# A decoder kernel on one core: an earlier load of k and q, and a chunk of attention scores split around two transposes

## The chip, the cores and the metric

One core of a Trainium2 chip runs the whole kernel. The metric is the device time of one execution in microseconds (us). A profiled execution adds a trace with the start and length of the instructions of each engine: TensorE (PE; its weight loads are PEld), VectorE (DVE), ScalarE (ACT), GpSimd (POOL) and the DMA queues of SyncE (SP, in rows SPq) and of ScalarE (ACTq). Times in rows count from the first instruction.

## What is computed

One decoder layer on x of 16 sequences x 256 tokens x 512, in float32. The first third is differential attention over the heads of one token (32 half-heads by 32, not over the sequence):

```
q = split(x @ Wq.T) * SCALE ; k = split(x @ Wk.T) ; v = heads(x @ Wv.T)
att = softmax(einsum('bnqd,bnkd->bnqk', q, k))
diff = att[:, :, :H, :H] - lam * att[:, :, H:, H:]
out = rms(einsum('bnah,bhnd->bnad', diff, v)) * (1 - LAM_INIT)
x = layernorm(x + out @ Wo.T + bo)
x = layernorm(x + x * scan(decay, ctx * ctx))
h = relu(x @ ternary(W_fc).T)**2 ; x = layernorm(x + rms_norm(h) @ ternary(W_proj).T)
```

The ternary weights (sign times a scale per group of 64) are also made in the kernel.

## The kernel before

The 4096 tokens are worked in 8 blocks of 512. The kernel has two phases; the change lies in the first, which takes the first 520 us or so. The second (output projection, scan, feed-forward) runs from then on.

**The first phase** is a software pipeline written out by hand, one list of steps for each engine, in `body(i, do_2, do_1)`: body 0 and 1 are written out, bodies 2 to 7 run as a loop (on SyncE the last one is written out too). In body i TensorE projects block i into q, k and v, computes the scores of block i-1, and mixes the values of block i-2. Beside these it transposes the ternary weights: part 0 (W_fc) of body i behind projections 8 and 9, part 1 (W_proj) at the start of body i+1. Engines wait on semaphores only.

TensorE's body, by the lines: `x_transpose(i, t)` (L531) transposes token tile t of x, for t of 0 to 3, into a bank of PSUM. There are two banks, used in turn, so tiles 2 and 3 wait until tiles 0 and 1 have been taken out: by ScalarE (`x_upper`, L837, the high part `xth`) and by VectorE (`x_lower`, L1040, the low part `xtl`). In L541 and L542 transpose t waits for the high and low parts of tile t-2. `scores(i, c, first, end)` (L565) does chunk c of four: for each of 32 groups a small matmul of k with a block-diagonal q (`qbd`). Chunks 0 and 1 need the first half of q, 2 and 3 the second; chunk 0 also needs k. A chunk fills two banks, and `s_ps` (L582) tells of it per column strip, at the chunk's last eighth group (gq == 7). `w_transpose(i-1, 1, 0)` (L604) waits for the low part of x tile 2. `project(i, n)` (L547) for n of 0 to 11 is 12 matmuls each; projection 0 waits for all four low parts.

The order in TensorE's body (L622) is transposes 0 and 1, score chunk 0, transposes 2 and 3, weight transpose, projection 0 with chunk 1 inside it, and so on; chunks 2 and 3 stand behind projections 5 and 7.

**The way of q and k.** ScalarE copies each projection out of PSUM (`f_copy`, L844) and writes it to DRAM from its own queue: q chunks are n of 0 to 3, k chunks 4 to 7, v chunks 8 to 11. The copy of chunk n waits for the write of chunk n-3. SyncE loads them back in another layout: `first_half_load(i)` (L397) holds until the scores of block i-1 are done (`s_ps`) and chunks 0, 1, 5, 6 and 7 are written, then issues one load of k (L387, 1 MB) and eight of q (L382, 64 KB each). `second_half_load` (L403) brings the rest of q.

**The way of the weights.** `w_in` is one buffer, filled twice in a body: with W_fc (L428, L436) and with W_proj (L441). The second fill has to wait until the weight transposes behind projections 8 and 9 have read the first. ScalarE's `w_round(i, 1)` (L874) reads it at the end of the body, behind the copy of chunk 11: absolute values to `w_b` (L880), then signs. VectorE's `w_signs(i, 1)` (L1128; L1142 to L1151) is the last step of its body (L1185), behind the softmax of chunk 3 and the turn of the difference. The next in its queue is `x_lower(i+1, 0)`. GpSimd multiplies (L1439).

**SyncE's body** (L424): the loads of the difference for block i-2, of the next x, of the second half of q, of W_fc, the writes of W_proj's transposes, the load of v; then, in L440 to L442, the hold for the weight transposes, the load of W_proj into `w_in` and `first_half_load(i)`; then the writes of W_fc's transposes (L445) and of o. A hold stops SyncE, and all that is behind it waits. Each issue takes its own time on SyncE.

Of the kernel before, what the change touches and what calls it, by code (L numbers as in the profile page):

```python
# [58 lines left out]
def at(i, per, k):  # L59

    return i * per + k
# [7 lines left out]
def later(i):  # L69

    return not (isinstance(i, int) and i == 0)
# [15 lines left out]
def program(nc, x_in, ctx_in, wq, wk, wv, wo, bo, lq1, lq2, lk1, lk2, decay, w_fc, w_proj, out):  # L87
# [15 lines left out]
    with ExitStack() as stack:  # L103
# [189 lines left out]
        FULL = G // 2  # L293
# [12 lines left out]
        def x_bank(t):  # L306

            return ps_t[:] if t % 2 == 0 else ps_f[:, 0, :]
# [41 lines left out]
        def _(sp):  # L350
# [15 lines left out]
            def hold(*waits):  # L366


                for n, (signal, value) in enumerate(waits):
                    if n and not isinstance(value, int):  # L370
                        sp.sem_inc(passed, 1)
                    sp.wait_ge(signal, value)
                if not isinstance(waits[-1][1], int):
                    sp.sem_inc(passed, 1)

            def f_written(i, chunks):

                return [(f_wr[n % 3], at(i, 64, 16 * (n // 3 + 1))) for n in chunks]

            def q_load(i, s):  # L380
                for t in range(LANES):
                    sp.dma_start(qbd[H * t:H * (t + 1), lane_slot(t), :, :],  # L382
                                 q_scr[i, s * 256:(s + 1) * 256, t * G:(t + 1) * G]
                                 .rearrange("(d a) g -> d a g", a=H)).then_inc(qbd_ld, 16)

            def k2_load(i):
                sp.dma_start(k2[:], k_scr[i].rearrange("t (d h) g -> (t d) h g", h=2 * H)).then_inc(k2_ld, 16)  # L387

            def v2_load(i):
                hold(*([(av_ps, at(i, 16, 0))] if later(i) else []),  # L390
                     *f_written(i, (9, 10, 11)))
                for t in range(LANES):
                    at_t = H * (2 * (t % 4) + t // 4)
                    sp.dma_start(v2[at_t:at_t + H, :, :],
                                 v_scr[i, t].rearrange("(h e) g -> h e g", e=HD)).then_inc(v2_ld, 16)

            def first_half_load(i):  # L397

                hold((s_ps, at(i, 16, 0)) if later(i) else (zeroed, 2), *f_written(i, (0, 1, 5, 6, 7)))
                k2_load(i)  # L400
                q_load(i, 0)

            def second_half_load(i):  # L403
                hold((s_ps, at(i, 16, 8)), *f_written(i, (2, 3)))
                q_load(i, 1)

            def dbd_load(i):

                hold((d_tr, i + 1))
                for t in range(LANES):  # L410
                    sp.dma_start(dbd[H * t:H * (t + 1), t, :, :],
                                 dt[H * t:H * (t + 1), :, :]).then_inc(dbd_ld, 16)

            def o_write(i):
                hold((o_done, at(i, 4, 4)))
                sp.dma_start(o_scr[i].rearrange("t (a e) g -> (t a) e g", e=HD), o_sb[:]).then_inc(o_wr, 16)

            def w2_write(i):
                for r in range(2):
                    hold((wt_ev, at(i, 4, r + 3)))  # L420
                    sp.dma_start(w2_scr[:, bass.ds(i * 2 + r, 1), :],
                                 w_st[:, r:r + 1, :]).then_inc(wt_wr[r], 16)

            def body(i, do_2, do_1, last=False):  # L424
                if do_2:
                    dbd_load(i - 2)
                if not later(i):
                    sp.dma_start(w_in[:].rearrange("p (r d) -> p r d", d=D), fc_t[i]).then_inc(wt_ld, 16)  # L428
                if not last:
                    hold((xt_ps, at(i, 4, 4)))  # L430
                    sp.dma_start(xa[:], x_t[i + 1]).then_inc(xa_ld, 16)
                if do_1:
                    second_half_load(i - 1)
                if later(i):
                    hold((wt_ps, at(i, 4, 0)))
                    sp.dma_start(w_in[:].rearrange("p (r d) -> p r d", d=D), fc_t[i]).then_inc(wt_ld, 16)  # L436
                    w2_write(i - 1)
                if do_1:
                    v2_load(i - 1)
                hold((wt_ps, at(i, 4, 2)))  # L440
                sp.dma_start(w_in[:].rearrange("p (b n) -> p b n", b=4), proj_t[i]).then_inc(wt_ld, 16)  # L441
                first_half_load(i)  # L442
                for r in range(2):
                    hold((wt_ev, at(i, 4, r + 1)))
                    sp.dma_start(w1_scr[:, :, bass.ds(i * 256 + r * P, P)],  # L445
                                 w_st[:, r, :].rearrange("p (k h) -> p k h", k=KC)).then_inc(wt_wr[r], 16)
                if do_2:
                    o_write(i - 2)

            body(0, False, False)  # L450
            body(1, False, True)
            with sp.Fori(2, NSB - 1) as i:
                body(i, True, True)
# [62 lines left out]
        def _(pe):  # L516
# [14 lines left out]
            def x_transpose(i, t):  # L531

                if t == 0:
                    pe.wait_ge(xa_ld, at(i, 16, 16))
                    if later(i):
                        pe.wait_ge(wt_ev, at(i - 1, 4, 2))
                elif t == 1:
                    if later(i):
                        pe.wait_ge(f_ev, at(i - 1, 12, 11))
                else:  # L540
                    pe.wait_ge(xt_hi, at(i, TT, t - 1))  # L541
                    pe.wait_ge(xt_lo, at(i, TT, t - 1))  # L542
                for k in range(KC):
                    last = nc.tensor.transpose(x_bank(t)[:, k * P:(k + 1) * P], xa[:, t, k * P:(k + 1) * P], ident[:])
                last.then_inc(xt_ps, 1)
# [19 lines left out]
            def scores(i, c, first, end):  # L565

                if first == 0:
                    if c % 2 == 0:
                        pe.wait_ge(qbd_ld, at(i, 256, 128 * (c // 2 + 1)))
                    if c == 0:  # L570
                        pe.wait_ge(k2_ld, at(i, 16, 16))
                    if c >= 2 or later(i):
                        pe.wait_ge(s_y, at(i, 4, c - 1))
                for n in range(first, end):
                    gq, j = n // 4, n % 4
                    g = j * 16 + (c % 2) * 8 + gq
                    last = nc.tensor.matmul(ps_s[32 * j:32 * (j + 1), 2 * (c % 2) + gq // 4,  # L577
                                                 (gq % 4) * P:(gq % 4 + 1) * P],
                                            k2[:, :, g], qbd[:, :, :, g].rearrange("p a b -> p (a b)"),
                                            start=True, stop=True)  # L580
                    if gq == 7:
                        last.then_inc(s_ps, 1)  # L582
# [39 lines left out]
            def body(i, do_2, do_1):  # L622
                x_transpose(i, 0)
                x_transpose(i, 1)
                if do_1:
                    scores(i - 1, 0, 0, FULL)
                x_transpose(i, 2)
                x_transpose(i, 3)
                if later(i):
                    w_transpose(i - 1, 1, 0)  # L630
                for n in range(12):
                    def beside(k):
                        if do_1 and n == 0 and k == 1:
                            scores(i - 1, 1, 0, FULL)

                    project(i, n, beside)
                    if do_2 and 1 <= n <= 4:
                        mix(i - 2, n - 1, 0, G // 4)
                    if do_1 and n in (5, 7):
                        scores(i - 1, n // 2, 0, FULL)  # L640
                    if n in W_FIRST:
                        w_transpose(i, 0, W_FIRST.index(n))
                    if n == W_SECOND and later(i):
                        w_transpose(i - 1, 1, 1)

            phase_a(pe, body)


# [838 lines left out]
```

## Time and profile before

| | us |
|---|---|
| median of 3 runs | 1276.65 |
| lowest, highest | 1274.16, 1279.75 |
| the profiled execution | 1274.55 |
| its span, first to last instruction | 1272.7 |
| TensorE matmuls busy | 1100.6 (86%) |
| VectorE busy | 939.4 (74%) |
| ScalarE busy | 587.1 (46%) |
| mean granted TensorE clock | 0.94 of full |

The time outside of the span is 1.85 us. Busy times are sums over the span, and say nothing on which wait ends last; for that one goes to the waits and the timelines of one body. A wait is put down to the releaser that came last. The granted clock of TensorE has two levels, 1.2 GHz (0.5) and 2.4 GHz (1.0); the mean of a stretch tells how much of it was at which.

### The profile page before, as it was taken

How to read it: one execution, taken by the hardware profiler on the slowest of the kernel's cores; microseconds unless marked ns; L12 is line 12 of the kernel's file. 1: busy time of each engine (PE TensorE's matmuls, PEld its weight loads, DVE VectorE, ACT ScalarE, POOL GpSimd, SP SyncE). 2: the span in 40 equal slices, each digit the busy share in tenths (PEclk: the TensorE clock that was granted, in tenths of full speed). 3: DMA queues.
4: the chain of work that ended last, by engine and by line, in shares of the span. 5: the costliest groups of instructions: out<-in, count | busy, mean ns of one | idle time of the engine just before them, and what ended most of it. 6: DMA issues, size and time to landing. Idle time of an engine off the chain costs nothing.

```text
span 1272.7 us, 22077 instructions
## 1 busy us (share of the span) xinstructions
PE 1100.6 (86%) x7424; PEld 873.7 (69%) x7424; DVE 939.4 (74%) x1932; ACT 587.1 (46%) x906; POOL 205.9 (16%) x202
## 2 busy tenths in 40 slices
PE   5988989889797979635599998998989989899995
PEld 4766767667575757424378787787877878778784
DVE  4287878787878888786858677696785867958746
ACT  4333333333243333310346555566555655655683
POOL 3100030303131312132140103003030030210000
PEclk9999999999898989767599999999999999999998
DMA  7566475766657565983530021201211012100001
GB/s 278 158 175 160 140 163 174 157 186 137 200 120 221 100 183 117 290 215 113 193 100 34 1 67 67 66 10 56 66 66 53 13 66 66 66 1 2 34 1 66
DMA packets 184334, 139.32 MB, mean 109 GB/s; under 512 B 140128, under 2 KB 152416, under 8 KB 180192
## 3 DMA queue, kind: packets, MB, share of 16 engines
q1 hardware_dynamic: 113120, 113.57, 31.8%
q10 hardware_dynamic: 71168, 25.17, 8.2%
q8 instruction: 25, 0.41, 0.1%
q14 instruction: 21, 0.17, 0.0%
HBM read 82.09 MB, written 52.43 MB: 106 GB/s over the span
## 4 chain that ended last, share of the span: by engine, by line
PE 66%; DVE 9%; ACT 7%; issue 7%; SPq 5%; DMA 4%; POOL 1%; ACTq 0%; DVEq 0%; POOLq 0%
PE ps_f L558 18%; PE ps_s L744 14%; PE ps_f L728 12%; PE ps_s L577 9%; PE ps_o L679 6%; DMA qbd<-q_scr 3%; SPq L382 3%; PE ps_o L597 2%; ACT h_sb L947 2%; DVE h_acc L1279 1%; ACT r_sb L941 1%; PE ps_t L619 1%; PE ps_f L679 1%; DMA w_raw<-in_L_attn_Wv 1%; ACT oth L919 1%
## 5 line engine op out<-in xcount | busy, mean ns | idle before, releaser
L728 PE MATMUL ps_f<-x2h,w 128*128 128x512 f32 x512 | 204.7, 400 | 1.6 <-DVE x2l L1260 1.6
L744 PE MATMUL ps_s<-w,hh 128*128 128x512 f32 x500 | 201.5, 403 | 0.0
L728 PE MATMUL ps_f<-x2l,w 128*128 128x512 f32 x512 | 200.7, 392 | 0.0
L744 PE MATMUL ps_s<-w,hl 128*128 128x512 f32 x500 | 199.3, 399 | 0.0
L1268 DVE TENSOR_TENSOR hl<-h_sb,hh 128x512 fp32r<-128x512 f32 x128 | 91.1, 712 | 112.2 <-ACT hh L951 110.5
L577 PE MATMUL ps_s<-qbd,k 128*32 128x128 f32 x2048 | 125.4, 412 | 55.0 <-DMA qbd<-q_scr 55.0
L558 PE MATMUL ps_f<-xth,wh 128*128 128x512 f32 x384 | 157.0, 409 | 1.6 <-DVE xtl L1044 1.6
L558 PE MATMUL ps_f<-xth,wl 128*128 128x512 f32 x384 | 150.3, 391 | 0.0
L558 PE MATMUL ps_f<-xtl,wh 128*128 128x512 f32 x384 | 149.8, 390 | 0.0
L577 PEld LDWEIGHTS ps_s<-qbd,k 128*32 128x32 f32 x2048 | 83.4, 149 | 91.9 <-issue 48.7
L1453 POOL TENSOR_TENSOR xb<-xb,bob 128x512 f32<-128x512 f32 x32 | 71.8, 2274 | 434.9 <-DMA xb<-in_x 434.9
L941 ACT ACTIVATE r_sb<-ps_f 128x512 f32<-128x512 f32 x128 | 76.2, 595 | 136.7 <-PE ps_f L728 136.5
L728 PEld LDWEIGHTS ps_f<-x2h,w 128*128 128x128 f32 x512 | 96.9, 189 | 21.1 <-issue 1.9
L744 PEld LDWEIGHTS ps_s<-w,hh 128*128 128x128 f32 x500 | 96.8, 194 | 19.9
L744 PEld LDWEIGHTS ps_s<-w,hl 128*128 128x128 f32 x500 | 96.7, 193 | 19.8
L728 PEld LDWEIGHTS ps_f<-x2l,w 128*128 128x128 f32 x512 | 96.8, 189 | 19.1
L959 ACT ACTIVATE h_sq<-h_sb 128x512 f32<-128x512 f32 x128 | 79.3, 620 | 55.3 <-DVE h_acc L1279 55.3
L851 ACT ACTIVATE f_sb<-ps_f 128x512 f32<-128x512 f32 x64 | 38.8, 606 | 135.9 <-PE ps_f L558 135.9
L558 PEld LDWEIGHTS ps_f<-xth,wh 128*128 128x128 f32 x384 | 72.1, 188 | 26.7 <-issue 11.9
L1439 POOL TENSOR_TENSOR w_in<-w_in,w_pos 128x512 f32<-128x512 f32 x32 | 37.6, 1196 | 291.3 <-DVE w_pos L1149 291.3
L947 ACT ACTIVATE h_sb<-r_sb 128x512 f32<-128x512 f32 x128 | 80.9, 632 | 6.4 <-ACT r_sb L941 2.8
L558 PEld LDWEIGHTS ps_f<-xth,wl 128*128 128x128 f32 x384 | 72.1, 188 | 16.1
(142 smaller groups left out, 1918.8 us busy)
## 6 DMA issues: line engine op xcount, KB each, us to landing
xa<-in_x SPq DMA_DIRECT2D x8, 1024.0 KB, 5.4
q_scr<-f_sb ACTq DMA_DIRECT2D x32, 256.0 KB, 2.6
k_scr<-f_sb ACTq DMA_DIRECT2D x32, 256.0 KB, 2.8
v_scr<-f_sb ACTq DMA_DIRECT2D x32, 256.0 KB, 5.7
k<-k_scr SPq DMA_DIRECT2D x8, 1024.0 KB, 7.5
qbd<-q_scr SPq DMA_DIRECT2D x128, 64.0 KB, 4.8
w_scr<-w_st SPq DMA_DIRECT2D x32, 256.0 KB, 4.9
v<-v_scr SPq DMA_DIRECT2D x64, 128.0 KB, 6.0
```

Source lines behind the costliest of these rows:

```text
L382: sp.dma_start(qbd[H * t:H * (t + 1), lane_slot(t), :, :], q_scr[i, s * 256:(s + 1) * 256, t * G:(t + 1) * G] .rearrange("(d a) g -> d a g ...
L558: last = nc.tensor.matmul(ps_f[:, n % 2, :], w[:, n // 4, k, cols], xx[:, k, :], start=(k == 0 and xx is xth and w is wh), stop=(k == KC - ...
L577: last = nc.tensor.matmul(ps_s[32 * j:32 * (j + 1), 2 * (c % 2) + gq // 4, (gq % 4) * P:(gq % 4 + 1) * P], k2[:, :, g], qbd[:, :, :, g].re ...
L679: last = nc.tensor.matmul(proj_bank(i, t), a[:, k, rows], w[:, k, :], start=(k == 0 and w is woh and a is oth), stop=(k == KC - 1 and a is ...
L728: last = nc.tensor.matmul(ps_f[:, j % 2, :], w1[:, k, j * P:(j + 1) * P], xx[:, k, :], start=(k == 0 and xx is x2h), stop=(k == KC - 1 and ...
L744: last = nc.tensor.matmul(ps_s[:, t, :], a[:, j % 4, t * P:(t + 1) * P], w2[:, j, :], start=(j == 0 and a is hh), stop=(j == HC - 1 and a ...
L851: nc.scalar.activation(f_sb[:, n % 3, :], ps_f[:, n % 2, :], ACT.Copy).then_inc(f_ev, 1)
L941: nc.scalar.activation(r_sb[:], ps_f[:, j % 2, :], ACT.Relu).then_inc(r_done, 1)
L947: nc.scalar.activation(h_sb[:, j % 4, :], r_sb[:], ACT.Square).then_inc(h_done, 1)
L959: nc.scalar.activation(h_sq[:, j % 2, :], h_sb[:, j % 4, :], ACT.Square).then_inc(hq_done, 1)
L1268: nc.vector.tensor_tensor(hl[:, j % 4, :], h_sb[:, j % 4, :], hh[:, j % 4, :].bitcast(F32), ALU.subtract).then_inc(hl_done, 1)
L1453: nc.gpsimd.tensor_tensor(xb[:, t, :], xb[:, t, :], bob[:], ALU.add).then_inc(xb_bias, 1)
```

## The change

SyncE issues the load of k and q (its hold included) ahead of the hold for the weight transposes and of the second load of `w_in`. TensorE does score chunk 0 in two halves of 16 groups: one ahead of x transposes 2 and 3, the other behind them. No instruction is added or removed.

```diff
@@ -437,9 +437,9 @@
                     w2_write(i - 1)
                 if do_1:
                     v2_load(i - 1)
+                first_half_load(i)
                 hold((wt_ps, at(i, 4, 2)))
                 sp.dma_start(w_in[:].rearrange("p (b n) -> p b n", b=4), proj_t[i]).then_inc(wt_ld, 16)
-                first_half_load(i)
                 for r in range(2):
                     hold((wt_ev, at(i, 4, r + 1)))
                     sp.dma_start(w1_scr[:, :, bass.ds(i * 256 + r * P, P)],
@@ -623,9 +623,11 @@
                 x_transpose(i, 0)
                 x_transpose(i, 1)
                 if do_1:
-                    scores(i - 1, 0, 0, FULL)
+                    scores(i - 1, 0, 0, FULL // 2)
                 x_transpose(i, 2)
                 x_transpose(i, 3)
+                if do_1:
+                    scores(i - 1, 0, FULL // 2, FULL)
                 if later(i):
                     w_transpose(i - 1, 1, 0)
                 for n in range(12):
```

## Rows read from the trace of the kernel before

**Rows 1.** Waits, bodies 2 to 7 (118 to 470 us): total, times, longest.
```profile
PE ps_s L577 <- DMA qbd<-q_scr: 39.6, 6, 7.5
...
PE ps_t L619 <- DVE xtl L1044: 7.1, 6, 1.3
```

**Rows 2.** TensorE, body 5: start us, us, what, idle before and its releaser.
```profile
299.18 3.92 PE L577 MATMUL ps_s<-qbd,k 128*32 128x128 f32 x64
...
315.02 0.60 PE L544 MATMUL ps_t<-ident,xa 128*128 128x128 f32 x4
315.46 0.60 PE L544 MATMUL ps_f<-ident,xa 128*128 128x128 f32 x4
323.61 3.92 PE L577 MATMUL ps_s<-qbd,k 128*32 128x128 f32 x64 [7.55 <-DMA qbd<-q_scr]
327.46 0.94 PE L544 MATMUL ps_t<-ident,xa 128*128 128x128 f32 x4
...
330.06 0.65 PE L619 MATMUL ps_t<-ident,w_in 128*128 128x128 f32 x4 [1.23 <-DVE xtl L1044]
```

**Rows 3.** Timeline of VectorE, body 5, same columns.
```profile
319.13 1.18 DVE L1142 TENSOR_REDUCE gsum<-w_b 128x16 f32<-128x1024 bf16 x1
...
324.28 0.69 DVE L1044 TENSOR_TENSOR xtl<-ps_t,xth 128x512 fp32r<-128x512 f32 x1
...
329.13 0.69 DVE L1044 TENSOR_TENSOR xtl<-ps_t,xth 128x512 fp32r<-128x512 f32 x1 [3.57 <-ACT xth L841]
```

**Rows 4.** Timeline of ScalarE, SP and ACT queues, end of body 4.
```profile
300.09 0.38 ACTq L860 DMA_DIRECT2D k_scr<-f_sb  x1
...
309.94 0.40 SPq L441 DMA_DIRECT2D w_in<-in_L_ffn_W_proj  x1
...
311.24 0.35 SPq L387 DMA_DIRECT2D k<-k_scr  x1
...
311.68 7.30 SPq L382 DMA_DIRECT2D qbd<-q_scr  x8
...
316.40 1.06 ACT L880 ACTIVATE w_b<-w_in 128x1024 bf16<-128x1024 f32 x1 [0.58 <-ACT f_sb L853]
```

**Rows 5.** DMA issues of 240 to 370 us: KB each, median us to landing.
```profile
k<-k_scr SPq DMA_DIRECT2D x2, 1024.0 KB, 8.1
...
k_scr<-f_sb ACTq DMA_DIRECT2D x8, 256.0 KB, 2.8
...
w_in<-in_L_ffn_W_fc SPq DMA_DIRECT2D x2, 512.0 KB, 5.0
```

**Rows 6.** Timeline, end of body 0 and start of body 1.
```profile
48.88 0.38 ACTq L860 DMA_DIRECT2D k_scr<-f_sb  x1
...
55.61 6.24 SPq L382 DMA_DIRECT2D qbd<-q_scr  x8
...
62.32 1.22 DVE L1142 TENSOR_REDUCE gsum<-w_b 128x16 f32<-128x1024 bf16 x1 [17.57 <-ACT w_b L880]
...
69.87 0.66 PE L544 MATMUL ps_t<-ident,xa 128*128 128x128 f32 x4
```

**Rows 7.** Timeline of TensorE, body 7, transposes 2 and 3.
```profile
459.49 1.11 PE L544 MATMUL ps_t<-ident,xa 128*128 128x128 f32 x4
460.40 0.99 PE L544 MATMUL ps_f<-ident,xa 128*128 128x128 f32 x4
```

**Rows 8.** Three stretches: us, engines busy, PEclk (granted clock), DMA share, GB/s.
```profile
300.00:310.00 10.00, 10.00 (x90) 7.71 (x83) 8.62 (x13) 2.91 (x4) 5.78 (x13) 1.00 0.23 52
321.00:328.00 7.00, 4.39 (x67) 3.23 (x68) 4.56 (x18) 0.00 (x0) 2.36 (x2) 0.52 0.98 299
328.00:331.00 3.00, 1.77 (x13) 1.44 (x12) 1.87 (x3) 1.26 (x3) 0.00 (x0) 0.99 0.43 75
```

**Rows 9.** Timeline of TensorE behind the loop.
```profile
526.35 1.09 PE L619 MATMUL ps_t<-ident,w_in 128*128 128x128 f32 x4 [1.68 <-POOL w_in L1439]
```

**Rows 10.** Chain that ended last, behind the loop: start us, us, what.
```profile
526.95 3.82 SPq L459
```

## The prediction, made before the changed kernel was run

> **What bounds the kernel now.** I read first who waits for whom in the six full bodies (2 to 7) [rows 1]: TensorE stands 39.6 us for q, six times, and 7.1 us for the low part of x before the weight transpose. Those 46.7 us, 7.8 us a body, are all that the change aims at.
>
> TensorE's timeline of body 5 shows where they lie [rows 2]. The second x transpose ends at 316.06 (315.46 + 0.60), the first score chunk starts at 323.61 after 7.55 us of idling for q, transposes 2 and 3 follow from 327.46 on, then 1.23 us idle, then the weight transpose at 330.06, with projection 0 behind it. From there TensorE has no gap until the next body's transposes. So what the change can move is what lies between the end of transpose 1 and the weight transpose: 14.0 us here.
>
> VectorE's timeline of the same stretch decides the case [rows 3]. It is not idle while TensorE is: from 319.13 on it makes the weights' signs; only then, at 324.28, does it make the low part of x tile 0, and right behind it that of tile 1. Transpose 2 waits for the first of these and transpose 3 for the second. Before the change the score chunk stood between, and neither wait showed.
>
> **Part 1, the load of k and q ahead.** Its hold (for the load at the end of body 4) needs the write of k chunk 7, issued at 300.09 [rows 4]; writes of k land in a median of 2.8 us [rows 5], so at 302.9. It also needs the last score chunk, which TensorE runs right behind projection 7, so at about the same time. Between the issue for w_in and that for k SP took 0.90 us for the holds (309.94 + 0.40 to 311.24), so with some 0.2 us for these scores k goes out at about 304.0 instead of 311.24: 7.2 us earlier. The eight q issues take 7.30 us in this body, to 311.7. The old chain from k's issue to the chunk's start was 12.4 us (311.24 to 323.61), so q is there at 316.4, when TensorE ends transpose 1 (316.06). The wait for q is gone, or 0.3 us of it is left.
>
> What is moved past: w_in's second load was issued at 309.94 and now stands behind nine issues, at about 311.8, with 1.5 MB in front of it. The nearest row is the first w_in load, issued right behind eight q loads: 5.0 us to landing [rows 5], so 316.8. ScalarE began to read w_in at 316.40 [rows 4] and its result (1.06 us) was ready at 317.46, but VectorE took it up only at 319.13 [rows 3]. There is 1.67 us of slack, and 0.4 is used: I cost this at nothing in bodies 2 to 7. The bounds are nothing (it can't gain, being issued later) and 1.8 us a body if w_in takes the 8.1 us that k takes [rows 5]. The weight writes and the write of o behind it on SP were held by q's issues before and are released as early or earlier. In the ACT queue, the write of v chunk 8 now runs beside k's load; the copy of chunk 11 waits for it, within the same slack.
>
> In body 1 the slack isn't there [rows 6]: VectorE stood idle for 17.57 us until ScalarE had read w_in, so it started the signs at 62.32. SP can start k at 51.7 there (48.88 + 2.8), the q issues take 6.24 us, w_in goes out at 58.3 and lands at 63.3; read in 1.1 us, it lets the signs start at 64.4, 2.1 us later. x tile 0's low part ends 5.84 us behind their start in body 5 (319.13 to 324.97), so at 70.3. Transpose 2 moves from 69.87 to about 70.5, and what stands between it and the weight transpose grows from 2.6 us (body 5: 327.46 to 330.06 [rows 2]) to 3.86 (1.9 us for the transposes at the low clock, told below, and 1.96 for the half chunk): 0.6 + 1.3 = **+1.9 us**. If w_in lands in the 2.8 us of a k write, it is about 0.
>
> **Part 2, the halves.** A chunk is 3.92 us [rows 2], so a half is 1.96. New body 5: first half 316.1 to 318.0; then TensorE waits for the low part of tile 0, done at 324.97 (324.28 + 0.69), plus 0.24 us, which is what passed between such an end (329.82) and the weight transpose (330.06). Idle: 325.2 - 318.0 = 7.2 us. VectorE's chain hangs on TensorE's projection 10 by way of ScalarE, so I take it as the same in all six bodies. The second half now covers the low parts of tiles 2 and 3, and the 1.23 us wait goes. At an equal clock: 6 x 7.2 = 43.2 us of idling against 46.7, less 0.1 us a body for transpose 3, which waits for tile 1: **-2.9 us**. The wait for q is thus not removed; VectorE takes it over almost whole.
>
> The clock then takes that back. The windows show it near half (0.52, the 1.2 GHz level) from 321 to 328 us and full (2.4 GHz) behind [rows 8]: it was low after TensorE had idled some 5 us, and back 4.5 us after it resumed. Before, the work done at the low clock was mostly scores, and a chunk of those takes 3.92 us at either level (at 323.61, and at 299.18 [rows 2] with the clock full [rows 8]). Now the idling lies directly ahead of transposes 2 and 3. Body 7 shows their price at the low clock: 459.49, 460.40, end 461.39, so 1.9 us for the pair [rows 7]; 1.04 us for transposes 0 and 1 at the full one (315.02 to 316.06 [rows 2]). That is +0.8; the weight transpose (0.65 us; 1.09 at the low clock [rows 9]) and the first matmuls of projection 0 come 3.8 us after resumption, when the clock may or may not be back: +0.35, some half of the full price. Six bodies: 6.9, less 1.2 that is paid already (body 7's pair 0.86, body 5's transpose 2 with 0.94 instead of 0.60, 0.34): **+5.7 us**.
>
> The Trainium skill has a rule that speaks against this placing (TensorE: Matmul & The Clock Gate, section "HAM oscillation"): a short burst of matmuls in front of a long wait doesn't keep the clock up, and the work behind the wait starts cold every time. By it the sum is as told; without it 5.7 us less. The trace agrees in body 5, with its 0.52.
>
> **Behind the loop.** The last score chunk 0 also stops waiting for q, but what follows it waits for GpSimd's weights (1.68 us, until 526.35 [rows 9]) and then for SP's long row of issues [rows 10]. These begin with the write of o, released by GpSimd, and no part of it is moved. The nearest stall that may ease, since k and q have landed earlier, is the 3.82 us issue at 526.95: bounds 0 and -1.9 (half of it). I take **-0.7 us**. The second phase runs the same instructions.
>
> **Sum:** 1.9 - 2.9 + 5.7 - 0.7 = +4.0 us. The profiled execution took 1274.55 us (span 1272.7), so 1278.6 by its own time; it lies 2.1 us under the median of 1276.65, and on the median the forecast is **1280.6 us**, 0.3% slower. Effects under 0.5% (6.4 us) are about what a measurement of this kernel can't tell from no change.
>
> **The rivals.**
> *The clock costs nothing* (the half chunk shortens the cold stretch, or it ends before the transposes). For it: it was back in body 5 by the time of the second of these transposes. Then body 1 costs 1.1, and the sum is -2.9 + 1.1 - 0.7 = -2.5: 1274. With body 1 at no cost and the whole of the bound behind the loop, -4.8: 1272.
> *w_in becomes the wait* (the other side, slower). Place: SP's second w_in load, read by ScalarE, on which VectorE's signs hang, and on those transposes 2 and 3. It decides from the point where w_in lands later than 318.1 in body 5 (316.40 + 1.67). At k's 8.1 us it lands at 319.9: 1.8 us late, six times 10.8 us, and in body 1 3.1 more: 1276.65 + 4.0 + 10.8 + 3.1 = 1295; half of that lateness gives 1288. Against it: w_in has half of k's bytes.
> [...]
> *VectorE is not in the way* (the waits for x's low parts come earlier than I read, so that the stalls really go). Then only the 2.4 us from a transpose to the end of its low part (327.46 to 329.82) would stay in each body, and 46.7 - 14.4 = 32 us would go: 1244. Against it stands the order of VectorE's queue; what is open is a partial form of 7 to 10 us, by shorter queues in the DMA rings and behind the loop: 1268.
> *It doesn't do what it says:* q's load is as late as before, because its hold is released by something later. Then part 2 alone acts: 1277.
>
> **How the numbers follow.** Forecast as told (1275 to 1284): 0.50. Clock without cost: 0.20. w_in late: 0.13. Gain beyond 6.4 us: 0.09. No effect: 0.08. Faster than 1270.3 is the fourth case and a part (0.03) of the second: 0.12. Slower than 1283.0 is the third with 0.11, and the upper edge of the first with 0.05: 0.16. The rest, 0.72, is within 0.5%. The range of 8 in 10 leaves out most of the fourth case and the upper half of the third: 1269 to 1288.
>
> **What would show it.** Right: k issued some 7 us earlier in each body; no wait of TensorE for q in bodies 2 to 7, but six of about 7 us on the low part of x (transpose 2, from VectorE); the low clock still there in each body, with transposes 2 and 3 at 0.9 to 1.1 us; VectorE's signs at the same distance behind projection 10; body 1's signs 2 us later. Wrong: VectorE idle ahead of the signs in bodies 2 to 7 with ScalarE's reading of w_in as releaser (the w_in rival); transposes 2 and 3 at 0.6 us (the clock rival); TensorE's idle under 5 us a body; or q still named as what ends the waits.

## The result, and the profile after

| | before | after |
|---|---|---|
| median of 20 runs, us | 1274.88 | 1278.24 |
| lowest, highest | 1271.75, 1279.75 | 1275.07, 1283.25 |
| profiled execution (span) | 1274.55 (1272.7) | 1282.61 (1280.8) |

The ratio is 1.0029, with a 95% interval of 1.0015 to 1.0042: the change makes the kernel 0.29% slower, some 3.7 us. The forecast was 0.31% (+4.0 us), as a median 1280.6 us; the median of before from 20 runs lies 1.8 us under that of the 3 runs it started from. The runs of either kernel spread over some 8 us, twice the effect, and in both 9 of the 20 lie above a gap in the list (1275.06 to 1276.42 us before, 1278.31 to 1280.29 after), so what parts them weighs alike in both medians.

TensorE's waits in bodies 2 to 7 (118 to 474 us), in the view that [rows 1] are from. No wait for q is left in them, and the one on x's low part has taken its place:

```profile
PE ps_t L544 <- DVE xtl L1046: 42.2, 6, 7.1
```

TensorE's timeline of body 5, to be read beside [rows 2]:

```profile
324.74 0.60 PE L544 MATMUL ps_f<-ident,xa 128*128 128x128 f32 x4
325.27 2.07 PE L577 MATMUL ps_s<-qbd,k 128*32 128x128 f32 x32
334.40 1.09 PE L544 MATMUL ps_t<-ident,xa 128*128 128x128 f32 x4 [7.05 <-DVE xtl L1046]
335.28 1.06 PE L544 MATMUL ps_f<-ident,xa 128*128 128x128 f32 x4
336.27 2.07 PE L577 MATMUL ps_s<-qbd,k 128*32 128x128 f32 x32
338.27 1.12 PE L619 MATMUL ps_t<-ident,w_in 128*128 128x128 f32 x4
```

The first half chunk starts right behind transpose 1 (325.34), so q is there in time. Then TensorE stands for 7.05 us, where it stood for 7.55 and 1.23. Transposes 2 and 3 take 1.94 us together (334.40 to 336.34). From the end of transpose 1 to the weight transpose there are 12.9 us, against 14.0 before. Body 5 flatters the change, since q had been latest there. Counted from the end of transpose 1 and summed over bodies 2 to 7, transpose 2 starts 8.4 us earlier than before (54.3 us against 62.6), but the weight transpose no earlier (77.5 against 77.4), and projection 0 starts 0.5 us later (81.0 against 80.5).

VectorE's timeline of the same stretch, beside [rows 3]:

```profile
328.42 1.18 DVE L1144 TENSOR_REDUCE gsum<-w_b 128x16 f32<-128x1024 bf16 x1
...
333.57 0.69 DVE L1046 TENSOR_TENSOR xtl<-ps_t,xth 128x512 fp32r<-128x512 f32 x1
```

The signs start 3.08 us behind the end of transpose 1, as before (3.07), and x tile 0's low part 5.15 us behind them, also as before. VectorE's chain has not moved by a tenth; it is only visible now.

The queues and ScalarE at the end of body 4, beside [rows 4], and the landings of the same stretch, beside [rows 5]:

```profile
309.38 0.38 ACTq L862 DMA_DIRECT2D k_scr<-f_sb  x1
...
313.30 0.35 SPq L387 DMA_DIRECT2D k<-k_scr  x1
...
313.74 5.84 SPq L382 DMA_DIRECT2D qbd<-q_scr  x8
...
319.94 0.40 SPq L442 DMA_DIRECT2D w_in<-in_L_ffn_W_proj  x1
...
325.69 1.11 ACT L882 ACTIVATE w_b<-w_in 128x1024 bf16<-128x1024 f32 x1 [0.58 <-ACT f_sb L855]
```

```profile
k<-k_scr SPq DMA_DIRECT2D x2, 1024.0 KB, 5.4
...
w_in<-in_L_ffn_W_proj SPq DMA_DIRECT2D x2, 512.0 KB, 5.0
```

k goes out 3.92 us behind the write of chunk 7, where it took 11.15: 7.2 us earlier. w_in goes out 5.4 us ahead of the end of transpose 1 (before: 6.1) and takes 5.0 us, as taken from the load behind eight q loads. ScalarE reads it with the same gap behind its own work as before (0.58), so w_in isn't waited for.

**The clock.** Stretches of the changed kernel, columns as in [rows 8]; the third and fourth are the idling and what follows it in body 5:

```profile
22.00:32.00 10.00, 7.30 (x24) 5.62 (x23) 2.80 (x5) 2.24 (x4) 7.50 (x2) 0.51 1.00 359
325.00:329.00 4.00, 2.35 (x36) 1.35 (x33) 3.70 (x6) 3.25 (x5) 1.27 (x1) 1.00 0.73 176
329.40:339.60 10.20, 5.20 (x45) 4.09 (x46) 7.83 (x25) 1.32 (x3) 2.27 (x2) 0.50 0.70 195
339.60:342.00 2.40, 2.40 (x26) 1.68 (x28) 2.30 (x4) 0.51 (x1) 0.00 (x0) 0.99 0.68 265
```

It was low from 329.4 to 339.6 us, over both transposes, the second half chunk and the weight transpose (1.12 us where it was 0.65). In bodies 2, 5 and 7 the weight transpose took 1.12 us, in bodies 3, 4 and 6 0.66: there the clock was back in time. The first row explains a difference of another kind. In this execution the clock was also low from 22 to 32 us, in body 0, where the two kernels do the same. In the profile of before it was full there:

```profile
22.00:32.00 10.00, 7.26 (x36) 5.68 (x35) 2.58 (x4) 2.75 (x6) 7.54 (x2) 1.00 1.00 357
```

That puts all of the changed kernel's profile 3.37 us late from the start of body 1 on, and is no work of the change: experiments 3 and 6 below run the same instructions up to the end of body 0, and the clock of this stretch was 1.00 in the profile of one and 0.50 in that of the other; transpose 1 of body 1 ended at 60.75 and at 64.11 us.

**Where the 8.06 us between the two profiled executions lie.** Rows of before (transpose 1 and the weight transpose of body 1, the weight transpose of body 7), then the same of after, with w_in's issue, ScalarE's reading and VectorE's signs between:

```profile
60.34 0.60 PE L544 MATMUL ps_f<-ident,xa 128*128 128x128 f32 x4
...
72.21 0.63 PE L619 MATMUL ps_t<-ident,w_in 128*128 128x128 f32 x4 [1.25 <-DVE xtl L1044]
...
462.27 0.66 PE L619 MATMUL ps_t<-ident,w_in 128*128 128x128 f32 x4 [0.88 <-DVE xtl L1044]
```

```profile
62.12 0.63 SPq L442 DMA_DIRECT2D w_in<-in_L_ffn_W_proj  x1
...
63.71 0.60 PE L544 MATMUL ps_f<-ident,xa 128*128 128x128 f32 x4
...
67.64 1.07 ACT L882 ACTIVATE w_b<-w_in 128x1024 bf16<-128x1024 f32 x1 [3.57 <-DMA w_in<-in_L_ffn_W_proj]
...
68.75 1.22 DVE L1144 TENSOR_REDUCE gsum<-w_b 128x16 f32<-128x1024 bf16 x1 [20.61 <-ACT w_b L882]
...
78.64 1.12 PE L619 MATMUL ps_t<-ident,w_in 128*128 128x128 f32 x4
...
470.53 1.12 PE L619 MATMUL ps_t<-ident,w_in 128*128 128x128 f32 x4
```

- Up to transpose 1 of body 1: 63.71 - 60.34 = 3.37, the clock of the start.
- From there to the weight transpose of body 1: 14.93 against 11.87, **+3.1** (forecast +1.9).
- From there to that of body 7: 391.89 against 390.06, **+1.8** (forecast -2.9 + 5.7 = +2.8). In the trace of experiment 3, whose bodies 2 to 7 are the same, it is 390.8, +0.8: a single trace gives this term to about 1 us.
- Behind it, to the end of the span: 810.27 against 810.43, **-0.2** (forecast -0.7).

The change's own part is +4.7 in these two executions, +3.7 by the ratio, +4.0 by the forecast.

### The profile page after: what moved, and what is told of

It reads as the page before. It is cut to its first block, busy times and chain, and to the rows that moved or that the text cites. A ratio compares the mean times of both kernels' runs of the same rounds, so it can differ in the third digit from the quotient of the medians.

```text
span 1280.8 us, 22077 instructions
## 1 busy us (share of the span) xinstructions
PE 1112.8 (87%) x7424; PEld 882.3 (69%) x7424; DVE 941.7 (74%) x1932; ACT 588.4 (46%) x906; POOL 207.1 (16%) x202
## 4 chain that ended last, share of the span: by engine, by line
PE 66%; DVE 13%; ACT 7%; issue 6%; SPq 2%; DMA 2%; POOL 1%; ACTq 0%; DVEq 0%; POOLq 0%
PE ps_f L558 19%; PE ps_s L746 14%; PE ps_f L730 12%; PE ps_s L577 8%; PE ps_o L681 6%; PE ps_o L597 2%; DVE w_pos L1151 2%; ACT h_sb L949 1%; DVE h_acc L1281 1%; ACT r_sb L943 1%; PE ps_t L619 1%; PE ps_f L681 1%; DMA w_raw<-in_L_attn_Wv 1%; SPq L382 1%; ACT oth L921 1%
```

## The experiments

The theory is the prediction's: q's wait is handed to VectorE, the low clock takes back what idling is saved, and body 1 pays for w_in. All ratios are against the kernel before, with their intervals; 0.1% is 1.3 us.

**1. Only SyncE's order.** `scores(i - 1, 0, 0, FULL)` stands ahead of transposes 2 and 3 again.

> Only SyncE's order changed, score chunk 0 whole. My theory (VectorE's low part of x tile 0 releases transpose 2, whatever stands before it): transpose 2 starts at the same distance behind transpose 1 as in the changed kernel (9.0 us), TensorE idles about 5 us there instead of 7, and since no half chunk stands behind transposes 2 and 3, projection 0 follows transpose 2 by 2.9 to 3.3 us instead of 4.3 to 4.6. Six bodies and body 1 gain 1.2 us each against the changed kernel: about 8 us, so some 1270, 0.4% under the kernel before. Rival (the split hides the evacuations and earns its place; the loss of the changed kernel comes from SyncE's order): slower than the changed kernel, 1280 or more.

Measured: 1.0031 (1.0013 to 1.0050), 1278.86 us. A miss by some 9 us, and the most useful one; its rival had put the loss on SyncE's order, and that part of it holds. TensorE's timeline of body 6, from transpose 2 on:

```profile
399.99 1.09 PE L544 MATMUL ps_t<-ident,xa 128*128 128x128 f32 x4 [5.21 <-DVE xtl L1044]
400.87 1.06 PE L544 MATMUL ps_f<-ident,xa 128*128 128x128 f32 x4
402.75 1.11 PE L619 MATMUL ps_t<-ident,w_in 128*128 128x128 f32 x4 [0.81 <-ACT xth L841]
403.51 0.77 PE L558 MATMUL ps_f<-xth,wh 128*128 128x512 f32 x1
404.08 0.63 PE L558 MATMUL ps_f<-xtl,wh 128*128 128x512 f32 x1
```

Transpose 2 starts 9.1 us behind the end of transpose 1 and the idling before it is 5.2 us, both as expected. Projection 0 starts 3.5 us behind transpose 2, where 2.9 to 3.3 were expected, and it starts at the low clock: matmuls follow each other by 0.43 us instead of 0.23, and chunk 1 (at 405.99) comes 6.0 us behind transpose 2. In the changed kernel the second half chunk, which doesn't mind the clock, runs meanwhile; projection 0 starts 0.8 us later, with its matmuls soon 0.23 us apart, and chunk 1 comes 5.9 us behind transpose 2 (406.69 against 400.84). My expectation kept the clock's price to the transposes. Which of the two pieces stands first is worth nothing here.

**2. Only the halves.** SyncE's two statements in their old order.

> Only the halves, SyncE's order as before. My theory: q is late as before, the first half starts at about 323.6 of body 5 and ends at 325.6, when the low part of tile 0 is ready in all bodies but for some tenths; transposes 2 and 3 run at the low clock, then the second half; projection 0 comes within 0.7 us of where it was: the whole within 4 us of the kernel before, no body 1 penalty. Rival (the halves cost by the low clock, 1 us a body): 1282.

Measured: 1.0000 (0.9982 to 1.0018), 1274.65 us; waits for q 39.8 us in six bodies, on x's low part 2.7. As expected. The halves alone cost and bring nothing, and with experiment 1, the loss comes with SyncE's order.

**3. Body 0 as before.**

```diff
-                first_half_load(i)
+                if later(i):
+                    first_half_load(i)
                 hold((wt_ps, at(i, 4, 2)))
                 sp.dma_start(w_in[:]..., proj_t[i]).then_inc(wt_ld, 16)
+                if not later(i):
+                    first_half_load(i)
```

> The change, but body 0 keeps w_in's second load ahead of the load of k and q. My theory: in body 1 the weights' signs start where they did in the kernel before, and projection 0 of body 1 comes about 3 us earlier than in the changed kernel; the rest of the trace is the same. About 1275.5, 3 us under the changed kernel. Rival (the late part in body 1 is made up for in body 2, or comes from the start's clock alone): no difference to the changed kernel.

Measured: 1.0010 (0.9992 to 1.0028), 1275.74 us. The signs of body 1 start at 62.14 us (before 62.32) and not at 68.75; 3.6 of these 6.6 us had passed by the end of transpose 1 (60.75 against 64.31), by the clock of the start, which was full in this execution, and the other 3.0 are the change's. The ratio lies 0.19% (2.4 us) under the changed kernel's; the intervals overlap, but the trace has the 3 us where they were expected.

**4. TensorE kept at work.** The first half of chunk 0 is done four times, writing the same values to the same place; three of the four are no part of the computation.

```diff
                 if do_1:
-                    scores(i - 1, 0, 0, FULL // 2)
+                    for _ in range(4):
+                        scores(i - 1, 0, 0, FULL // 2)
```

> The change, with the first half of chunk 0 done four times over (the same values to the same place), so that TensorE works for 7.8 of the 9 us between transposes 1 and 2. My theory of the clock: it stays at its full level through every body; transposes 2 and 3 take 1.1 us together instead of 1.9, the weight transpose 0.65 us, and projection 0 follows transpose 2 by 3.6 us instead of 4.3 to 4.6: 6 to 8 us under the changed kernel, about 1271. Rival (the low clock costs nothing here, what follows is bound by the evacuations): transposes faster, but projection 0 at the same distance, 1278.

Measured: 0.9983 (0.9967 to 0.9999), 1273.27 us, 0.46% (5.9 us) under the changed kernel's ratio. TensorE, body 5:

```profile
320.71 7.67 PE L577 MATMUL ps_s<-qbd,k 128*32 128x128 f32 x128
329.89 0.63 PE L544 MATMUL ps_t<-ident,xa 128*128 128x128 f32 x4 [1.50 <-DVE xtl L1047]
330.49 0.63 PE L544 MATMUL ps_f<-ident,xa 128*128 128x128 f32 x4
...
333.04 0.66 PE L619 MATMUL ps_t<-ident,w_in 128*128 128x128 f32 x4
```

Transposes 1.23 us for the pair, projection 0 3.56 us behind transpose 2. Transpose 2 comes no earlier (9.1 us behind transpose 1): only the clock has changed, and its mean over the bodies is 0.99. So 5.9 us (6 to 8 were expected), give or take 2.7, is what the low clock costs in the changed kernel, body 1 included.

**5. Filled, and body 0 as before.** Experiments 3 and 4 together.

> The filled kernel with body 0's order as before. If the clock and body 1 are two separate costs, they add up: 2.5 us under the filled kernel, some 1271, 0.35 to 0.4% under the kernel before. If both come by way of the same low stretch in body 1, no gain over the filled one (1273).

Measured: 1.0004 (0.9988 to 1.0020), 1276.70 us. A miss: they don't add up. TensorE, body 1:

```profile
69.34 7.67 PE L580 MATMUL ps_s<-qbd,k 128*32 128x128 f32 x128 [5.48 <-DMA qbd<-q_scr]
76.94 0.66 PE L547 MATMUL ps_t<-ident,xa 128*128 128x128 f32 x4
```

With body 0's old order q comes late in body 1, and the fill runs behind it, 5.8 us past the low part of x tile 0 (ready at 71.13). The fill is free only where something else is waited for.

**6. The same, the fill in bodies 2 to 7 only** (`range(4 if do_2 else 1)`).

> The filled kernel with body 0's order as before, and with the fill only in bodies 2 to 7. The filled kernel with body 0's order as before lost 5.8 us in body 1, where q landed late (69.3) and the fill of 7.8 us ran behind it, 5.8 us past the low part of x tile 0 (71.1 to 76.9). Without the fill there the two gains should add up: 1268 to 1272, 0.35 to 0.5% under the kernel before. Rival (the clock of the start decides): 1275.

Measured: 0.9968 (0.9953 to 0.9984), 1270.82 us. Now they add up. Against experiment 3, which differs by the fill in bodies 2 to 7 alone, it is 0.42% (5.4 us, give or take 3): the price of the low clock in these six bodies.

**7. w_in later still.** Its load behind the two writes of w1 as well.

> The change, with w_in's second load behind the two weight writes as well. Its landing in the changed kernel left 2.4 us of slack in body 5 (0.8 ahead of ScalarE's reading, 1.7 from its result to the signs). The load now goes out some 2 us later and behind 0.5 MB more: it lands 2.5 to 4 us later, so the slack is used up and 0 to 1.5 us a body come on the chain, and 2.5 to 4 us in body 1: 1281 to 1291. Rival (VectorE's chain does not hang on w_in): as the changed kernel.

Measured: 1.0036 (1.0017 to 1.0055), 1279.87 us, just under the expected 1281 to 1291. The upper rival of the prediction, forced. SP, ScalarE and VectorE in body 5:

```profile
323.46 0.50 SPq L446 DMA_DIRECT2D w_in<-in_L_ffn_W_proj  x1
...
327.73 1.11 ACT L882 ACTIVATE w_b<-w_in 128x1024 bf16<-128x1024 f32 x1 [1.08 <-DMA w_in<-in_L_ffn_W_proj]
...
329.99 1.18 DVE L1144 TENSOR_REDUCE gsum<-w_b 128x16 f32<-128x1024 bf16 x1
```

ScalarE now waits for w_in (9.1 us in six bodies), but the signs still start 3.1 us behind transpose 1 (326.89): VectorE is busy until then. Even with w_in's load some 2 us later, nothing comes on the chain in this body (0.3 us does in body 3): w_in had room there. In body 1, where it had none, the weight transpose comes 16.3 us behind transpose 1, against 14.3 in the changed kernel. The ratios differ by less than their intervals.

**8. The low parts first.** VectorE's order, with SyncE's of experiment 3:

```diff
                 for t in range(TT):
                     x_lower(i, t)
+                if later(i):
+                    w_signs(i - 1, 1)
...
                     diff_turn(i - 1)
-                w_signs(i, 1)

             phase_a(v, body)
+            w_signs(NSB - 1, 1)
```

On TensorE and ScalarE `w_transpose(i - 1, 1, 0)` and `w_copy(i - 1, 1, 0)` move behind projection 0.

> VectorE makes the low parts of the four x tiles ahead of the signs of the weights (which move into the next body), and the weight transpose stands behind projection 0; SyncE as in the change but for body 0. My theory (the wait on x's low parts is what keeps the stalls in): transpose 2 starts 4 us behind transpose 1 instead of 9, projection 0 some 6.5 us earlier per body; VectorE's softmax of chunk 0 then starts 5 us behind projection 0 instead of with it, and part of the gain comes back as waits of TensorE for the turns of the mix. 3 to 5 us a body, 20 to 35 us in all: 1240 to 1256. Rival (VectorE is the bound of the body, its order is all the same): no more than 5 us under the kernel before.

Measured: 1.0003 (0.9985 to 1.0022), 1277.58 us. The rival's outcome. The wait on the low part did shrink to 11.8 us in six bodies, but another one came. TensorE, body 4:

```profile
262.52 0.63 PE L547 MATMUL ps_t<-ident,xa 128*128 128x128 f32 x4 [2.03 <-DVE xtl L1049]
...
284.05 1.81 PE L600 MATMUL ps_o<-dbd,v 128*32 128x128 f32 x32 [2.87 <-DVE o_sb L1113]
...
286.38 0.63 PE L561 MATMUL ps_f<-xtl,wh 128*128 128x512 f32 x1
```

The mix of chunk 1 waits 2.87 us for VectorE's turn 0, which takes the results of the mix's chunk 0 out of PSUM and stands in VectorE's queue behind the first half of the softmax of two score chunks. Behind this wait the matmuls run at the low clock (0.43 us apart). Both waits together are 4.9 us in place of 7.05, and TensorE's busy time in this body rose from 57.9 (before) to 60.6 us.

**9. Reordered in another way.** As experiment 8, with chunk 0 whole, chunk 1 behind transposes 2 and 3, and only turn 0 moved ahead.

> As the kernel with the low parts first, with chunk 0 whole, chunk 1 right behind transposes 2 and 3 in place of inside projection 0 (it covers the evacuations of tiles 2 and 3), and the first turn of the mix ahead of the softmax of chunk 1. If the waits of TensorE for the turn of the mix are what is left, these 4 us a body go too: 5 to 15 us under the kernel with the low parts first, 1230 to 1245. Rival (VectorE's sum of work is the bound): no difference between the two.

Measured: 1.0057 (1.0037 to 1.0078), 1282.87 us. A miss. Two waits grew in bodies 2 to 7: to 15.8 us (from 14.1) for the turns of the mix and to 14.1 us (from 0.7) for GpSimd's weights. By my reading the second comes of projection 0, which has no chunk in it now, so that TensorE is early at the weight transpose; that was not tried by itself. VectorE's sum of work is not the bound: it is busy for 273.8 us of five bodies here and for 275.5 us in the next experiment, which is 30 us faster.

**10. The turns early.** Experiment 8 and all three turns ahead:

```diff
                     soft_first(i - 1, 0)
-                    soft_first(i - 1, 1)
...
                     mixed_turn(i - 2, 0)
...
-                    soft_second(i - 1, 0)
+                    soft_first(i - 1, 1)
...
                     mixed_turn(i - 2, 1)
...
-                    soft_second(i - 1, 1)
+                    soft_second(i - 1, 0)
...
                     mixed_turn(i - 2, 2)
+                if do_1:
+                    soft_second(i - 1, 1)
```

ScalarE's `exps(i - 1, 1)` moves behind the copy of projection 2.

> The kernel with the low parts first, with VectorE's turns of the mix moved ahead (turn 0 before the softmax of chunk 1, turn 1 before the second half of chunk 0, turn 2 before that of chunk 1) and ScalarE's exp of chunk 1 behind the copy of projection 2. In the kernel with the low parts first, what came back was TensorE's wait for turn 0 (2.9 us in body 4) and the low clock behind it (its busy time rose from 58 to 60.6 us). If that is what gave the gain back, TensorE's only wait left is 2 us on the low part of tile 0, and a body takes 61 to 63 us instead of 65.1: 1250 to 1262. Rival (VectorE and TensorE hand the chain to each other at other places too, so that the sum stays): within 4 us of the kernel before.

Measured: **0.9816 (0.9797 to 0.9835), 1252.58 us** (5 runs), 1.8% under the kernel before. TensorE's waits in bodies 2 to 7 are what was expected:

```profile
PE ps_t L547 <- DVE xtl L1049: 11.8, 6, 2.0
...
PE ps_o L600 <- DVE o_sb L1113: 4.4, 6, 0.7
...
PE ps_t L622 <- POOL w_in L1448: 1.8, 4, 0.6
```

**11. The same with SyncE's old order.** Is the change's first part worth anything?

> The kernel with the turns early, with SyncE's order as before the change (w_in's second load ahead of k and q in every body). My theory: what VectorE hid, shows now. q lands some 7.5 us behind transpose 1 again, so the first half chunk ends at 9.5 us and transpose 2 starts there instead of at 4.0: up to 5.5 us a body come back, less what VectorE has of slack: 1270 to 1288, so the early load is worth some 20 to 35 us in this order of VectorE and nothing in the old. Rival (the early load has no worth in either): 1253.

Measured: 1.0051 (1.0029 to 1.0073), 1283.62 us. TensorE, body 4:

```profile
265.45 2.07 PE L577 MATMUL ps_s<-qbd,k 128*32 128x128 f32 x32 [7.18 <-DMA qbd<-q_scr]
267.45 0.96 PE L544 MATMUL ps_t<-ident,xa 128*128 128x128 f32 x4
```

The low part of tile 0 was ready at 262.04; now q is what transpose 2 waits for, and the waits for q are 40.0 us again. The early load is worth 0.0235 of the time (some 30 us) with this order of VectorE, and nothing with the old one. The order has a price of its own: with the late load it is 0.5% slower than the kernel before. Five bodies, from the end of transpose 1 in body 2 to that in body 7, take 335.9 us against 328.7: 3.5 us less up to projection 0, and 10.8 us more behind it. These are there in experiment 10 too (10.7); part of them is the weight transpose, which stands behind projection 0 now, and the waits for the turns and for GpSimd's weights (6.8 us here).

**12. The same as experiment 10 with chunk 0 whole.**

> The kernel with the turns early, with chunk 0 whole ahead of transposes 2 and 3. Chunk 0 fills the 4 us up to the low part of tile 0 (TensorE's 2 us wait goes), but the evacuations of tiles 2 and 3 are bare (1.2 us): within 3 us of the kernel with the halves, either way, 1250 to 1256. Rival (the halves are what makes it fast): 1260 or more.

Measured: 0.9815 (0.9790 to 0.9840), 1252.44 us. The halves bring nothing here either.

## Why the prediction was right

- *q's wait is handed to VectorE almost whole.* Six waits of 7.0 us, where 7.2 were forecast, and no wait for q. The two hide each other, and a third stands behind them. The early load alone gave a loss (1.0029; 1.0010 with body 0 spared, experiment 3), VectorE's order alone a loss (1.0051, experiment 11), the early load with only the low parts moved nothing (1.0003, experiment 8), and the load with the low parts and the turns of the mix 1.8% (experiment 10).
- *The clock takes the gain back.* The whole price of the low clock in six bodies was forecast at 6.9 us, of which 1.2 were paid before: +5.7. A fill takes away the whole, so 6.9 is what to compare: 5.4 us by experiments 6 and 3, and 5.9 with body 1 in it by experiment 4, each give or take 3; in their traces, from the weight transpose of body 1 to that of body 7, 3.3 and 5.5 us. The term is of the right size, and if anything too high. Half of the full price for the weight transpose and the first matmuls was a guess, and it held: the weight transpose met the low clock in three bodies of six. The sum of both terms in bodies 2 to 7 was +2.8 in the forecast and +1.8 in the trace (+0.8 in that of experiment 3). The rival in which the clock costs nothing is out. It was priced at the transposes, rightly for this order; experiment 1 shows that the price turns up at projection 0 when no half chunk stands behind the transposes.
- *w_in costs nothing in bodies 2 to 7.* Right, and with more room than I gave it: k landed in 5.4 us instead of 8.1, and experiment 7 moved the load further without harm. That rival is out.
- *Body 1 pays.* Right in kind; the size was too small: +3.1 instead of +1.9. The eight q issues took 6.78 us instead of 6.24, and w_in was read 5.5 us behind its issue where 5.0 was taken. So the signs came 3.1 us later behind transpose 1 (4.4 against 1.4) and not 2.1. The last 0.3 us: from transpose 2 to the weight transpose body 1 took 2.3 us before, and not the 2.6 of body 5 that I used. By experiment 3 (2.4 us) the truth may lie between.
- *Behind the loop:* -0.7 was taken from half of a bound and -0.2 was seen. The 3.82 us issue took 3.71 us (at 535.75) in the changed kernel, so it was hardly waiting for k and q; for what it waits isn't shown.
- The sum came to +4.0 by terms of which body 1's was 1.2 too small, that of bodies 2 to 7 1.0 too high and that behind the loop 0.5 too low, against +4.7 in the two traces and +3.7 by the ratio. That these errors partly cancel is luck; the total is closer than the terms are.

What stays open: how much the clock at the start adds to a median. Some profiled executions have it low from 22 to 32 us and some not, and it moves all behind it by 3.4 us, nearly the whole effect of the change. Only one execution of each kernel was profiled, so how often it is low isn't shown. Open is also what the 10.8 us behind projection 0 in experiment 11 are made of, beyond the 6.8 us of waits.

## What to carry to other kernels

Before a wait is taken away, read what the waiting engine needs next and when that is ready: here, in body 5, x tile 0's low part came 1.4 us behind q (324.97 against 323.61), so of q's waits of 39.6 us in six bodies transpose 2 could gain 8.4 us at most, and in the changed kernel projection 0 kept none of it. Two waits that cover each other have to go in the same version; alone, each looks worthless. And a gap in TensorE's work has a second price in what stands right behind it, which here was worth 5 to 6 us. Work that doesn't mind the clock (here the score matmuls) can stand there at no loss, though it brought no gain here either (experiment 1); filling the gap did.

## What the runs showed of the hardware that was not expected

The 128-column score matmuls take the same time at either clock (2.07 us for 32 with the clock at 1.00 and at 0.50, body 5 of the changed kernel), whereas 512-column matmuls go from 0.23 to 0.43 us apart; and four transposes, also of 128 columns, from 0.60 to 1.09 us; so the low clock's price here depends on what meets it. A load of k (1 MB) landed in 5.4 us when w_in's 0.5 MB were queued behind it and in 8.1 us when they were queued ahead of it, with the same bytes in all. w_in itself went from 3.9 to 5.0 us. It is so in every kernel here: k's median over 240 to 370 us is 5.4 to 5.7 us in the eleven that issue it ahead of w_in, and 7.6 to 8.1 us in the three that don't. The order also moves the load in time, by 7.2 us; the two were not tried apart.
